# Cross-attention ahead of a transformer block: the next queries by VectorE and ScalarE, the next keys' turns placed ahead of the maxima, context in two alternating banks

## The reference

```python
h = layernorm(x)                                   # 16 x 64 x 512
scores = einsum('bsh,bqh->bsq', ctx, h)            # 16 x 1601 x 64
attn_weights = softmax(scores, axis=1)
x = x + einsum('bsq,bsh->bqh', attn_weights, ctx)
```

## Time and profile before

| | us |
|---|---|
| median of 3 runs | 842.59 (841.51 to 843.9) |
| span of the profiled execution | 837.9 |
| TensorE busy | 809.4 |
| VectorE busy | 516.9 |
| ScalarE busy | 309.8 |
| GpSimd busy | 306.3 |

### The profile page before, as it was taken

How to read it: one execution, slowest core, us unless ns; L and a number is a source line. 1 busy time by engine, 2 the same in 40 slices (tenths; PEclk the granted TensorE clock), 3 DMA queues, 4 the chain that set the end, 5 groups by cost and what they waited for, 6 DMA issues and landing times.

```text
span 837.9 us, 16088 instructions
## 1 busy us (share of the span) xinstructions
PE 809.4 (97%) x6110; PEld 599.1 (72%) x6111; DVE 516.9 (62%) x1160; ACT 309.8 (37%) x835; POOL 306.3 (37%) x152
## 2 busy tenths in 40 slices
PE   4899999999899999999999999999999999999996
PEld 3555455554557779888876777688888888888884
DVE  6878977797762345547688888864573344334334
ACT  4322233123353136763248575724323211121121
POOL 0000000000352625465021222244539999994034
PEclk9999999999999999999999999999999999999999
DMA  9958655773520040004059300040375565451138
GB/s 356 382 213 315 252 202 209 283 307 121 214 101 1 1 148 6 1 5 129 7 193 385 121 0 1 1 151 1 126 264 198 196 189 181 138 187 51 50 102 274
DMA packets 46570, 127.02 MB, mean 152 GB/s; under 512 B 4001, under 2 KB 8353, under 8 KB 40369
## 3 DMA queue, kind: packets, MB, share of 16 engines
q1 hardware_dynamic: 36752, 105.50, 34.6%
q10 hardware_dynamic: 7200, 12.32, 4.2%
q0 software_dynamic: 2560, 8.39, 3.0%
HBM read 102.05 MB, written 24.15 MB: 151 GB/s over the span
## 4 chain that ended last, share of the span: by engine, by line
PE 88%; DVE 4%; DMA 2%; POOL 2%; issue 1%; ACT 1%; SPq 0%; DVEq 0%; ACTq 0%; POOLq 0%
PE bank L614 11%; PE scores L581 11%; PE bank L1133 6%; PE bank L1135 6%; PE bank L1134 6%; PE bank L671 2%; POOL picked L1369 2%; PE bank L842 2%; PE bank L746 2%; PE bank L673 2%; PE bank L672 2%; PE bank L848 2%; PE bank L843 2%; PE bank L748 2%; PE bank L747 2%; PE bank L778 2%
## 5 line engine op out<-in xcount | busy, mean ns | idle before, releaser
L1823 DVE STREAM_TRANSPOSE ctxT<-nat 128x1024 f32<-128x1024 f32 (+3 forms) x124 | 116.8, 1003 | 0.8 <-DMA nat<-in_ctx_keys 0.7
L614 PE MATMUL bank<-nat,probT 128*64 128x512 f32 (+1 forms) x416 | 96.0, 606 | 0.1
L581 PE MATMUL scores<-ctxT,hn 32*64 32x385 f32 (+5 forms) x2048 | 88.8, 487 | 1.4 <-issue 0.9
L1240 POOL TENSOR_TENSOR wq_lo<-wq_raw,wq_hi 128x1024 fp32r<-128x1024 f32 x4 | 9.5, 2399 | 220.6 <-ACT wq_hi L1455 220.6
L1356 POOL TENSOR_TENSOR ring_lo<-ring_raw,ring_hi 128x2048 fp32r<-128x2048 f32 x18 | 83.0, 4612 | 14.5 <-ACT ring_hi L1711 13.3
L581 PEld LDWEIGHTS scores<-ctxT,hn 32*64 32x64 f32 x2048 | 63.1, 131 | 24.0 <-issue 13.9
L1133 PE MATMUL bank<-ring_hi,xg_lo 128*128 x180 | 74.2, 412 | 0.0
L1135 PE MATMUL bank<-ring_hi,xg_hi 128*128 x180 | 70.6, 392 | 0.0
L1134 PE MATMUL bank<-ring_lo,xg_hi 128*128 x180 | 70.1, 389 | 0.0
L614 PEld LDWEIGHTS bank<-nat,probT 128*64 128x64 f32 (+1 forms) x416 | 29.5, 138 | 53.9 <-issue 52.5
L2459 DVE TENSOR_TENSOR rhm_lo<-bank,rhm_hi 128x512 fp32r<-128x512 f32 x21 | 14.5, 692 | 79.6 <-ACT rhm_hi L1722 79.6
(11 more groups left out here) (314 smaller groups left out, 1920.3 us busy)
## 6 DMA issues: line engine op xcount, KB each, us to landing
nat<-in_ctx_keys SPq DMA_DIRECT2D x48, 1024.0 KB, 7.3
ring_raw<-in_Wexp SPq DMA_DIRECT2D x21, 1024.0 KB, 6.4
x_slots<-zeros SPq DMA_DIRECT2D x1, 5632.0 KB, 18.3
y_slots<-zeros SPq DMA_DIRECT2D x1, 5632.0 KB, 32.8
hn<-x_slots ACTq DMA_DIRECT2D x22, 256.0 KB, 4.6
y_slots<-hn ACTq DMA_DIRECT2D x22, 256.0 KB, 3.0
w_raw<-in_Wexp SPq DMA_DIRECT2D x3, 1024.0 KB, 5.6
nat<-in_ctx_keys SPq DMA_DIRECT2D x16, 130.0 KB
```

Source lines behind the costliest of these rows:

```text
L581: last = nc.tensor.matmul(scores4[64 * b:64 * b + 64, i, 0:keys_in[i]], q4[rows_i, j, 64 * b:64 * b + 64], ctxT[rows_i, b, j, 0:keys_in[i] ...
L614: last = nc.tensor.matmul(bank[7][64 * b:64 * b + 64, :], probT[0:n, j, 64 * b:64 * b + 64], nat[k % 2][0:n, b, j, :], start=j == 0, stop= ...
L1823: dve.transpose(dst, src).then_inc(columns_ready, 1)
```

## The change

Four things are changed, all in the first stage.

- Queries of steps 2 to 7. ScalarE writes the normed rows once, as 128x512 (`spread_queries`), into a part of `prob`; VectorE turns them there in 32x32 blocks (`turn_queries`); ScalarE then copies the blocks to the four groups of 32 partitions in 16 copies on 32 partitions each. Even steps have their queries in `qn`, odd steps in `q4`. TensorE no longer turns them. Steps 0 and 1 stay as they were. The norms' factors are computed for tiles 2 and 3 together and for 4 to 7 together.
- Keys. `keys_columns(k + 1, 0, (0, 1, 2))` stands before `maxima(k)`, and each chunk waits for the scores' own chunk by `scores_part`, which replaces `scores_full`. Chunk 3 stands after the maxima. Half 1 is turned around the query turn.
- Context. Even steps sum in bank 6, odd ones in bank 7, so `context(k, 0)` waits for the `finish` of step k - 2. Fill 3 of the probabilities uses bank 5. In TensorE's order fill 3 of the context of step k - 1 follows the first two turns of probabilities, and the fourth turn stands before context fill 1.
- SyncE issues piece 2 after context fill 2 and piece 3 after fill 3.

```diff
 P_FILLS = -(-JT // 4)
-PROB_BANK = [4, 5, 4, 6]
+PROB_BANK = [4, 5, 4, 5]
 QUERY_BANK = [6, 4, 6, 5]
...
         scope.close()
+        qn_rows = prob[:, 0:HC, :].rearrange("p t (j a) -> p (t j) a", a=B32)
+        q_blocks = prob[:, HC:2 * HC, :].rearrange("p t (j e) -> p (t j) e", e=B32)
+        q_even = qn[:].rearrange("p j r a -> p j (r a)")
...
-            return 4 * k + (1 + HC if k > 0 else 0)
+            return 4 * min(k, 2) + (1 + HC if k > 0 else 0) + max(k - 2, 0)
+
+        def queries_of(k):
+
+            return q_even if k > 1 and k % 2 == 0 else q4
+
+        def context_bank(k):
+
+            return bank[7 if k % 2 else 6]
...
                 for p, (j0, j1) in enumerate(PIECES):
-                    sp.wait_ge(context_part, 3 * k + min(p, 2) + 1)
+                    sp.wait_ge(context_part, P_FILLS * k + p + 1)
                     load_piece(k + 2, k % 2, j0, j1)
-            sp.wait_ge(context_part, 3 * (NT - 1))
+            sp.wait_ge(context_part, P_FILLS * (NT - 1))
             sp.dma_start(wq_raw[:], Wq.rearrange("(c p) n -> p c n", p=P)).then_inc(w_loaded["wq"], 16)
...
                     pe.wait_ge(qt_act, evicted(1) + 2)
-                elif k > 1 and f == 1:
-                    pe.wait_ge(probT_dve, k)
-                elif k > 1 and f == 3:
-                    pe.wait_ge(probT_act, 3 * (k - 1) + 1)
                 for j in range(4 * f, 4 * f + 4):
...
             def scores(k):
-                pe.wait_ge(qt_act, evicted(k) + 4)
+                pe.wait_ge(qt_act, evicted(k) + (4 if k < 2 else 1))
+                queries = queries_of(k)
                 keys_in = FIRST_KEYS if k == 0 else KEYS_IN
...
                                 last = nc.tensor.matmul(scores4[64 * b:64 * b + 64, i, 0:keys_in[i]],
-                                                        q4[rows_i, j, 64 * b:64 * b + 64],
+                                                        queries[rows_i, j, 64 * b:64 * b + 64],
                                                         ctxT[rows_i, b, j, 0:keys_in[i]], start=j == 0, stop=j == NB - 1,
                                                         skip_group_check=True)
-                last.then_inc(scores_full, 1)
+                    last.then_inc(scores_part, 1)
...
                     pe.wait_ge(qt_act, evicted(1) + 4)
-                elif f >= 2 and k < NT - 1:
-                    pe.wait_ge(qt_act, evicted(k + 1) + f)
                 elif f == 2:
                     pe.wait_ge(probT_dve, k + 1)
+                elif f == 3 and k < NT - 1:
+                    pe.wait_ge(probT_act, 3 * k + 1)
                 for j in range(4 * f, min(4 * f + 4, JT)):
...
                     pe.wait_ge(probT_dve, k + 1)
-                    if k > 0:
-                        pe.wait_ge(y1_ready, k)
-                    else:
-                        pe.wait_ge(prob_ready, 3)
+                    if k > 1:
+                        pe.wait_ge(y1_ready, k - 1)
                     if k == NT - 1:
...
                     for b in range(2):
-                        last = nc.tensor.matmul(bank[7][64 * b:64 * b + 64, :], probT[0:n, j, 64 * b:64 * b + 64],
+                        last = nc.tensor.matmul(context_bank(k)[64 * b:64 * b + 64, :], probT[0:n, j, 64 * b:64 * b + 64],
                                                 nat[k % 2][0:n, b, j, :], start=j == 0, stop=j == JT - 1,
                                                 skip_group_check=True)
-                if f != 2:
-                    last.then_inc(context_part, 1)
+                last.then_inc(context_part, 1)
...
                     context(k - 1, 2)
-                    context(k - 1, 3)
-                if k == 0:
+                else:
                     for f in range(4):
...
                 prob_transposes(k, 0)
-                if k > 0:
-                    query_transposes(k + 1, 0)
                 prob_transposes(k, 1)
                 if k > 0:
-                    query_transposes(k + 1, 1)
-                    query_transposes(k + 1, 2)
+                    context(k - 1, 3)
                 context(k, 0)
-                if k > 0:
-                    query_transposes(k + 1, 3)
                 prob_transposes(k, 2)
+                prob_transposes(k, 3)
                 context(k, 1)
-                prob_transposes(k, 3)
             context(NT - 2, 2)
...
+            def spread_queries(k):
+                act.wait_ge(norm_ready, 3 if k < 4 else 6)
+                nc.scalar.activation(qn_rows, y[:, k, :].rearrange("p (j a) -> p j a", a=B32), ACT.Identity,
+                                     bias=nmr[:, k:k + 1], scale=rstd[:, k:k + 1]).then_inc(qn_ready, 1)
+                act.wait_ge(norm_ready, k + (2 if k < 4 else 3))
+                for g in range(4):
+                    for i in range(4):
+                        last = nc.scalar.copy(queries_of(k)[B32 * i:B32 * (i + 1), :, B32 * g:B32 * (g + 1)],
+                                              q_blocks[B32 * g:B32 * (g + 1)])
+                last.then_inc(qt_act, 1)
+
             def query_columns_out(k, f):
...
                 act.wait_ge(nmax_ready, k + 1)
+                if 0 < k < NT - 1:
+                    act.wait_ge(qt_act, evicted(k + 1) + 1)
                 keys_in = FIRST_KEYS if k == 0 else KEYS_IN
...
                 exps(k)
-                if k > 0:
-                    query_columns_out(k + 1, 0)
-                probs_out(k, 1)
-                if k > 0:
-                    for f in range(1, 4):
-                        query_columns_out(k + 1, f)
-                probs_out(k, 2)
-                probs_out(k, 3)
+                for f in range(1, P_FILLS):
+                    probs_out(k, f)
                 if k + 2 < NT:
-                    queries(k + 2)
+                    spread_queries(k + 2)
...
             def maxima(k):
-                dve.wait_ge(scores_full, k + 1)
+                dve.wait_ge(scores_part, HC * (k + 1))
                 keys_in = FIRST_KEYS if k == 0 else KEYS_IN
...
                 for c in chunks:
+                    if h == 0:
+                        dve.wait_ge(scores_part, HC * (k - 1) + c + 1)
                     for b in range(2):
...
-                dve.wait_ge(context_part, 3 * (k + 1))
-                dve.scalar_tensor_tensor(y[:, k, :], bank[7][:], rinv[:, 0:1], y[:, k, :], ALU.mult,
+                dve.wait_ge(context_part, P_FILLS * (k + 1))
+                dve.scalar_tensor_tensor(y[:, k, :], context_bank(k)[:], rinv[:, 0:1], y[:, k, :], ALU.mult,
                                          ALU.add).then_inc(y1_ready, 1)
...
             first_columns()
+            def turn_queries(k):
+                dve.wait_ge(qn_ready, k + 1)
+                dve.transpose(q_blocks, qn_rows).then_inc(norm_ready, 1)
+
             for k in range(NT - 1):
+                keys_columns(k + 1, 0, (0, 1, 2))
                 maxima(k)
-                keys_columns(k + 1, 0, (0,))
+                keys_columns(k + 1, 0, (3,))
+                probs_out(k)
                 if k > 0:
                     finish(k - 1)
-                probs_out(k)
-                keys_columns(k + 1, 0, (1, 2, 3))
-                if k > 0:
                     second_stats(k - 1)
                 denominators(k)
-                keys_columns(k + 1, 1, range(HC))
                 if k == 0:
+                    keys_columns(1, 1, range(HC))
                     dve.wait_ge(x_loaded[1], 3 * 16)
+                    first_norm(2, 4)
+                    turn_queries(2)
+                    continue
+                elif k == 1:
+                    first_stats(4, NT)
+                elif k == 2:
+                    first_factors(4, NT)
+                keys_columns(k + 1, 1, (0, 1))
                 if k + 2 < NT:
-                    first_norm(k + 2, k + 3)
+                    turn_queries(k + 2)
+                keys_columns(k + 1, 1, (2, 3))
             finish(NT - 2)
```

More of the change, by code:

```diff
@@ L350, in perceiver_kernel @@
         norm_ready, qn_ready, qt_full, qt_act = sem("norm_ready"), sem("qn_ready"), sem("qt_full"), sem("qt_act")
-        columns_ready, scores_full, nmax_ready, prob_ready = sem("columns_ready"), sem("scores_full"), sem("nmax_ready"), sem("prob_ready")
+        columns_ready, nmax_ready, prob_ready = sem("columns_ready"), sem("nmax_ready"), sem("prob_ready")
         probT_full, probT_act, probT_dve = sem("probT_full"), sem("probT_act"), sem("probT_dve")
         context_part, y1_ready = sem("context_part"), sem("y1_ready")
+        scores_part = sem("scores_part")
         dve_step = sem("dve_step")
@@ L652, in norm_transposes @@
                 pe.wait_ge(hn_ready, k + 1)
-                if k == 1:
+                if k == 0:
                     pe.wait_ge(y1_ready, NT - 1)
@@ L1948, in _ @@
             dve.tensor_copy(block_bf[:], cst[:, C_BLOCK:C_BLOCK + P].unsqueeze(1).broadcast_to([P, 4, P])).then_inc(consts_cast, 1)
-            dve.wait_ge(qt_full, turns(NT - 1) + 4)
```

(1 more changed line is left out.)

## The result

The changed kernel takes 883.2 us (median of 4 runs, 882.57 to 883.62) against 842.62; the ratio is 1.0479, with a 95% interval of 1.0452 to 1.0507. The profiled execution has a span of 881.5 us and took 883.31.

A forecast was written before the change was run, and what follows sets the result against it. TensorE, busy 97% of the span, was taken as the bound. Step 0's 7.5, longer periods' 15.9 and slower clock's 10.2 sum to 33.6 us: span 837.9 becomes 871.5, plus 4.7 around it, 876.2 us; range 861 to 889.

The forecast's parts named there:

- the case that I held likeliest: Whole kernel: the main forecast of 876.2 us, with its own range 870 to 883, chance 0.56.
- step 0: First step: VectorE waits for the second piece of keys 1, so context fill 0 starts 7.5 us later.
- the wait: Steps 1 to 6: key turns ahead of the maxima lengthen each period 2.65 us net of saved query turns, 15.9 in all.
- the clock: Steps 1 to 6: TensorE's clock drops after each new idle, 1.7 us per period (0 to 1.94), 10.2 in all.
- Landing at S + 9.4: Each steady step: the keys' second piece lands 9.4 us after S, the start of that step's scores.
- The rival of 7.6: Keys of each period land sooner, 7.6 us after first issue, from an emptier queue: 865.4 us, chance 0.12.
- Turns 6.87, maxima 2.14, exponential 0.81: Chain behind the landing: six key turns 6.87 us and maxima 2.14 on VectorE, then first exponential 0.81.
- A period of 29.5 without the clock: Steady step: next scores start 29.5 us after this step's, instead of 26.85, before any loss to a slower clock.
- the third rival: Keys land later, at 10.5 us, with clock loss 1.94 per period: 884.2 us or more, chance 0.10.
- 4.7 us around the span: Whole run: median time 842.59 exceeds the profiled span 837.9 by 4.7 us, added to the new span.
- The spread on ScalarE at nothing: ScalarE's 16 query copies, 9.9 us, fit before the next exponentials and cost nothing.
- Query turns, 12.5 us off TensorE: Six periods: query turns leave TensorE, 2.09 us each, a gain on offer of 12.5 us.

The follow-up runs named there:

- the filled kernel: Changed kernel plus five unused 128x512 matmuls behind context fill 2 in steps 1 to 6: 862.93 us, 1.0248 against the kernel before.
- The kernel without piece 1: Changed kernel without the transfers of the keys' second piece for steps 2 to 7, half 0 waiting for piece 0 only: 846.98 us, 1.0047.
- the keys alone: Kernel before with only three chunks of the next keys' half 0 moved ahead of the maxima, waiting on scores per chunk: 879.32 us, 1.0450.
- the best kernel: Changed kernel with one key chunk ahead, fill 3 behind fill 2, tile 2 loaded and normed early, half 1's first chunk before statistics: 835.99 us, 0.9920.

## Why the prediction was right, point by point

The forecast was 876.2 us in a range of 861 to 889, slower; 883.2 was measured. That is just above the 870 to 883 of the case that I held likeliest. The spans differ by 43.6 us where the sum has 33.6: step 0 gave 6.9 (forecast 7.5), the wait 15.3 (15.9), by the filled kernel's six periods of 181.25 us in all against 165.99, the clock 20.1 (10.2), and 1.3 lie behind scores(7) (nothing).

- **Where the time goes.** Right: VectorE waits for piece 1 ahead of the maxima, everything behind it is late, TensorE idles. The kernel without piece 1 and the keys alone on the kernel before show it from both sides.
- **Landing at S + 9.4.** Right within 0.4 on average: the turns began 9.3 to 10.8 us after the scores' start (63.19 against 53.9, 96.64 against 86.8). The rival of 7.6, from an emptier queue, was too early. The estimate of 6.8 from the Trainium skill (DMA: Bandwidth & Descriptors, section Anatomy of one DMA — SWDGE (gpsimd) path), whose fit is for transfers from GpSimd, was too early as well. VectorE kept its order: the scores of step 2 ended at 98.2, the maxima, queued behind the waiting turn, began at 103.5, and ScalarE and TensorE waited for them. The Trainium skill's rule of strict order on VectorE (TensorE: Matmul & The Clock Gate, section Architectural detail: the array is 16× 32×32, not 1× 128×128) agrees with that.
- **Turns 6.87, maxima 2.14, exponential 0.81.** Measured 6.88, 2.06 with the gaps (103.52 to 105.58) and 0.79 in the chain.
- **A period of 29.5 without the clock.** Right: with five extra matmuls, which keep the clock up, the periods of steps 1 to 5 are 29.2 to 30.3.
- **Step 0, 7.5.** 7.7 at context fill 0 (44.83 against 37.09). The slow stretch was there in both, and less of it fell on context fill 0 (4.85 us against 5.52), so 6.9 remain at scores(1). (The prediction's own terms, 41.5 + 3.04, give 44.5 and 7.4.)
- **The clock, 1.7 per period: mis-sized by half.** The mechanism was right, and it came in all six steps. But I took the length of the slow stretch from the one after the last maxima, 3.4 us; here it was 6.8 us in the window shown, and the context passes under it took 6.3 to 7.7 us instead of 4.45, with 1.97 for the turns. The comparison of 883.2 and 862.93 gives 20 us, 3.4 per period, well outside the 0 to 1.94 that I had given as bounds. In four of the six steps the stretch was 10.2 us; the third rival named such a case, "two slow stretches follow one another", without a price. These extra 10 us are the miss in the span (881.5 against 871.5).
- **4.7 us around the span: wrong.** The changed kernel's profiled run took 883.31 with a span of 881.5, so 1.8 lie around it. What I took for the rest was that the profiled run of before was a quick one. This hid 3 us of the miss above: the two errors go opposite ways, and that the time is off by 7.0 and not by 9.9 is luck.
- **The spread on ScalarE at nothing.** Right for the changed kernel (10.10 us of idle behind it). It is not free in a shorter period: 1 us is left in the best kernel, and in step 1 it was on the path of the three versions with one chunk or none ahead and without the early norm of tile 2.
- **Query turns, 12.5 us off TensorE.** Right as work, wrong as a gain: the keys alone, with the query turns left in, were no slower than the full change. I had counted the shorter period, but not that with these turns and context fill 3 in their old places the idle would be shorter and parted, and the clock would stay up in four steps of six. Nor did the rest of the change gain by itself: with the keys behind the maxima it took 857.16, because in step 1 the exponentials waited for the spread of tile 2, and from step 2 on the scores for half 1.

## What to carry to other kernels

Before work is moved ahead of a step on the critical path, ask when its data lands, not only when its buffer is free: on an engine that runs in order, one wait for a transfer ahead of the reduction delayed every engine behind it, and in the changed kernel one chunk ahead (whose end was to fall in the cover) was 10 us better than none where three were 26 worse. An idle stretch of TensorE of 4.1 to 5.5 us cost some 3.4 us more by the clock behind it, so a wait that can't be removed is better covered with work than left idle; that spreading it helps as well is only suggested, by one run. When a wait is removed, look in the new chain for the next transfer: here it was the smallest one, issued last.

## What the runs showed of the hardware

Idle matmul time has a price of its own: 4.3 us of matmuls whose results nobody reads made the kernel 20 us faster (883.2 to 862.9), because the granted clock stayed at 1.00 instead of falling to 0.51 (1.2 GHz) after each idle stretch. I had not expected the slow stretch to be as long as 6.8 us behind an idle one of 4.6, and in four of six steps it was 10.2. Idle of about 2.8 and 1.2 us, parted by work, left the clock up in four of six steps and not in the other two, with hardly a difference in the idle.

A copy on 32 partitions costs ScalarE as much as one on 128: 16 copies of 32x512 took 10.02 us, 0.63 each, where a 128x512 copy takes about 0.59 (that one reads from a bank, the 16 do not).

An extra matmul of 128x512 took 0.86 us (nine took 7.7), while eight context matmuls of the same size take 3.58, 0.45 each. The extra ones all write output partitions 0 to 63, the context matmuls alternate between 0 to 63 and 64 to 127. That this is the reason is not shown apart.
